# An attention block on one Trainium2 core: the masks of the probabilities' high and low parts in one GpSimd instruction for each key tile

## Chip, core and metric

The kernel runs on one core of a Trainium2 chip. The metric is the device time of one execution in microseconds (us), the median of the executions shown. The engines of the core are TensorE (PE in the rows, its weight loads PEld), VectorE (DVE), ScalarE (ACT), GpSimd (POOL) and SyncE (SP), which here only issues DMAs. Each works through its own program in order and waits for the others by semaphores.

## The reference

The block is a transformer layer with adaptive layer norm on x of shape (2, 1024, 512): attention with 32 query heads and 8 key heads of 128, rotary embedding and a sliding window of 128 keys, then a gated feed-forward part. The part that matters here:

```python
i = pos[:, None]
j = pos[None, :]
allowed = (j <= i) & (j > i - SLIDING_WINDOW)
scores = jnp.where(allowed[None, None, None], scores, neg)
attn = jax.nn.softmax(scores, axis=-1)
out = jnp.einsum('bhgqs,bshd->bqhgd', attn, v).reshape(B, S, N_Q_HEADS * HEAD_DIM)
```

## The kernel before

All matrix products are made in three passes: each fp32 operand is split into a high part, rounded to fp32r, and a low part, the rest; `mm3` (L276, L277, L278) multiplies high by high, high by low and low by high into one PSUM bank.

Attention is 16 **steps**, one for each batch and key head. A step is 8 **units**, one for each tile of 128 queries, with the 4 query heads of the group side by side (512 columns). Most steps run in a hardware loop whose body holds units 2 to 9; units 8 and 9 are units 0 and 1 of the next step. In unit u, TensorE does `scores(u)` (pS), `p_times_v(u-2)` (pAv), `trans(u-1)`, the transposes of the probabilities (pTr, L286), one or two projections of the next chunk of 512 tokens (`slot_jobs`, pP), `out_proj(u-2)` (pOp), and in units 3 and 7 `turn_v`, the transposes of V (pXx, L355). The work of a probability tile goes from engine to engine: TensorE scores, VectorE `merge` (L879 to L885), ScalarE `exps` (L641), GpSimd `normalise` (L1249), TensorE `trans`, ScalarE `p_hi` (L634, pT part 0), VectorE `p_lo` (L865, pT part 1), GpSimd `mask` (L1242, pm), TensorE `p_times_v`. ScalarE `result_hi` (L629) and VectorE `result_lo` (L860) split its product for `out_proj`.

A window of 128 keys covers two key tiles, so `mask` makes two copies of the probabilities: pm[:, 0] with the keys of the query's own tile up to the diagonal, pm[:, 1] with those of the tile before beyond it. Unit 0 has only the first. `pm` is [128, 2, 2, 4, 128] (tile, part, head, query), and `pT` is [128, 2, 4, 128] (part, head, query).

Beside this runs the rotary work of the coming chunk, a **job** for each of K, Q0 to Q3 and V. A rotary job is `swap` on ScalarE (L651, L652), `rope_cos` on VectorE (L895), `rope_sin` on GpSimd (L1255), `rope_sum` on VectorE (L901, both inputs in SBUF), `rope_hi` on ScalarE (L661) and `rope_lo` on VectorE (L912, both inputs in SBUF, counts the job into `j_done`). In units 3 and 7 the jobs' part of VectorE's program is: sum of Q2, sum of Q3, the reciprocal of the row sums (L890), low part of Q2, low part of Q3. `p_lo` stands right ahead of it. GpSimd's program in such a unit is `mask` and then `normalise`. The next unit of TensorE, 4 or 8, uses the new chunk, and its scores begin with

```python
f.wait(j_done, PER_J, JB - 1 + (6 if t >= CH else 0) + PER_J * (u // NT))
```

which is fulfilled by the low part of Q3. `split_weight` on VectorE (L1033) makes the low parts of the weights, also from two inputs in SBUF.

Of the kernel before, what the change touches and what calls it, by code (L numbers as in the profile page):

```python
# [24 lines left out]
P = 128  # L25
# [3 lines left out]
ALU = mybir.AluOpType  # L29
# [42 lines left out]
def adaln_block(nc, x, wq, wk, wv, wo, w12, b12, w3, b3, cond, wmod, cos, sin, x1_spill, out):  # L72
# [3 lines left out]
    G = wq.shape[1] // DH // NKV  # L76
# [9 lines left out]
    with ExitStack() as ctx:  # L86
# [7 lines left out]
        base = {}  # L94

        def sbr(name, shape, dt):
            base[name] = nc.sbuf_base
            return sb(name, shape, dt)
# [16 lines left out]
        pT = sbr("pT", [P, 2, G, P], F32R)  # L115
        pm = sbr("pm", [P, 2, 2, G, P], F32R)
# [1115 lines left out]
        def _(pool):  # L1232
            def mask(f, u):

                f.wait(u_plo, PER_U, u + 1)
                f.wait(u_av, PER_U, u)
                f.stand()
                for own in ((0, 1) if u % NT else (0,)):
                    for part in range(2):

                        sign, op = (1, ALU.is_ge) if own == 0 else (-1, ALU.is_gt)
                        last = nc.gpsimd.affine_select(out=pm[:, own, part], in_=pT[:, part], compare_op=op,  # L1242
                                                       fill=0.0, base=0, pattern=[[0, G], [sign, P]],
                                                       channel_multiplier=-sign)
                last.then_inc(u_mask, 1)

            def normalise(f, u):
# [26 lines left out]
            def unit_step(f, u, b, jobs, prev=True):  # L1274
                if prev:
                    mask(f, u - 1)
                normalise(f, u)
                jobs()
                if u == 4:
                    side_rstd(f)  # L1280
# [22 lines left out]
            def residual_bias(i):  # L1303
# [3 lines left out]
                else:  # L1307
# [10 lines left out]
                                    pattern=[[-1, P]], channel_multiplier=1).then_inc(s_const, 1)  # L1318
            nc.gpsimd.affine_select(out=rA[:, 2, 0:P], in_=rA[:, 2, 0:P], compare_op=ALU.is_ge, fill=0.0, base=0,
                                    pattern=[[-1, P]], channel_multiplier=1).then_inc(s_const, 1)  # L1320
            nc.gpsimd.affine_select(out=rA[:, 2, P:2 * P], in_=rA[:, 2, P:2 * P], compare_op=ALU.is_gt, fill=0.0,
                                    base=0, pattern=[[1, P]], channel_multiplier=-1).then_inc(s_const, 1)
# [21 lines left out]
            for b in range(B):  # L1344
# [19 lines left out]
                for u in range(2, NT):  # L1364
# [7 lines left out]
                    if b == 0 and u >= 4:  # L1372
                        clear_y(u - 4)
            fl = Frame(pool, STEPS)
            mask(fl, -1)
            finish(fl, -2, 1)
            finish(fl, -1, 1)
# [218 lines left out]
```

## Time and profile before

| | before |
| --- | --- |
| median of 3 runs | 1507.73 us (1504.65 to 1507.94) |
| profiled execution: time | 1505.94 us |
| profiled execution: span of its instructions | 1504.1 us |
| TensorE matmul busy | 1476.1 us (98%) |
| VectorE busy | 1103.5 us (73%) |
| GpSimd busy | 868.4 us (58%) |
| ScalarE busy | 823.2 us (55%) |
| masks on GpSimd (L1242) | 480 instructions, 392.3 us |

The profiled execution took 1.8 us more than its span. Busy times are unions of the instructions' own spans; consecutive instructions of one engine overlap in the records by some hundredths of a us. An instruction that has been started and waits for a port is counted as busy, so a long duration can hold a wait.

### The profile page before, as it was taken

Reading aid. Unit: us, or ns where it says so; the run is one execution under the profiler, and the core shown is the slowest. Engines: PE = TensorE matmul, PEld = TensorE weight load, DVE = VectorE, ACT = ScalarE, POOL = GpSimd, SP = SyncE. Lnnn points to the kernel's source line nnn. Section 1 sums busy time; section 2 is a strip of 40 time slices with the busy share of each in tenths; the row PEclk is TensorE's granted clock in tenths of the full one; section 3 lists DMA queues with packets and bytes.
Section 4 is the critical chain, followed back from the end, with each engine's and each line's share of the span. In section 5 each row is a group of like instructions: output and inputs, shape, how many; then the busy total and the mean of one; then the engine's idle time right before and its main releaser. Section 6 shows DMA issues by size and latency. Waiting matters only on the chain.

```text
span 1504.1 us, 27328 instructions
## 1 busy us (share of the span) xinstructions
PE 1476.1 (98%) x7577; PEld 1227.3 (82%) x7577; DVE 1103.5 (73%) x1849; ACT 823.2 (55%) x2183; POOL 868.4 (58%) x894
## 2 busy tenths in 40 slices
PE   6989999999999999999999999999999999999998
PEld 4578888888888888887888888888888888877887
DVE  6678787778787878788777878787877868773542
ACT  3555565656555656555565655565655556552331
POOL 2346565556565566669855656556664665675333
PEclk9999999999999999999999999999999999999999
DMA  9011110020201111324302020111111101153001
GB/s 315 21 36 57 36 56 28 18 73 7 72 18 56 35 56 35 104 71 134 106 16 77 7 70 21 56 35 56 35 56 35 56 28 38 60 182 127 28 29 56
DMA packets 98688, 90.20 MB, mean 60 GB/s; under 512 B 5450, under 2 KB 73042, under 8 KB 98646
## 3 DMA queue, kind: packets, MB, share of 16 engines
q1 hardware_dynamic: 97718, 87.06, 18.4%
q0 software_dynamic: 640, 2.10, 0.4%
q10 hardware_dynamic: 288, 0.53, 0.1%
q8 instruction: 21, 0.34, 0.1%
q14 instruction: 21, 0.17, 0.0%
HBM read 74.98 MB, written 14.69 MB: 60 GB/s over the span
## 4 chain that ended last, share of the span: by engine, by line
PE 87%; issue 4%; DVE 4%; POOL 3%; ACT 1%; DMA 1%; SPq 0%; POOLq 0%; DVEq 0%; ACTq 0%
PE pP L276 11%; PE pP L278 11%; PE pP L277 11%; PE pOp L276 8%; PE pOp L278 7%; PE pOp L277 7%; PE pS L278 4%; PE pAv L276 4%; PE pS L277 4%; PE pS L276 4%; PE pAv L277 4%; PE pAv L278 4%; PE pTr L286 3%; PE pXx L355 1%; POOL y L1310 1%
## 5 line engine op out<-in xcount | busy, mean ns | idle before, releaser
L1242 POOL TENSOR_SCALAR_AFFINE_SELECT pm<-pT 128x512 fp32r<-128x512 f32 x480 | 392.3, 850 | 477.8 <-DVE pT L865 477.7
L276 PE MATMUL pP<-hT,wp 128*128 128x512 f32 (+1 forms) x776 | 314.5, 405 | 6.9 <-DVE hT L998 4.0
L278 PE MATMUL pP<-hT,wp 128*128 128x512 f32 (+1 forms) x776 | 303.3, 391 | 0.0
L277 PE MATMUL pP<-hT,wp 128*128 128x512 f32 (+1 forms) x776 | 302.3, 390 | 0.0
L629 ACT CAST oT<-pAv 128x512 fp32r<-128x512 f32 x128 | 74.9, 585 | 283.8 <-PE pAv L278 283.8
L1255 POOL TENSOR_TENSOR rB<-rB,tab 128x512 f32<-128x512 f32 x160 | 218.3, 1376 | 16.3 <-ACT rB L652 16.2
L641 ACT ACTIVATE pr<-pS,nb 128x128 f32<-128x128 f32 x512 | 181.4, 371 | 63.3 <-DVE nb L885 63.2
L895 DVE TENSOR_TENSOR rA<-pP,tab 128x512 f32<-128x512 f32 x160 | 110.3, 689 | 131.0 <-ACT rB L652 131.0
L276 PE MATMUL pOp<-wos,oT 128*128 128x512 f32 x512 | 201.4, 393 | 3.7 <-DVE oT L860 3.4
L278 PE MATMUL pOp<-wos,oT 128*128 128x512 f32 x512 | 199.6, 390 | 0.0
L277 PE MATMUL pOp<-wos,oT 128*128 128x512 f32 x512 | 199.3, 389 | 0.0
L276 PEld LDWEIGHTS pP<-hT,wp 128*128 128x128 f32 x776 | 147.1, 190 | 33.5 <-DVE hT L998 4.1
L278 PEld LDWEIGHTS pP<-hT,wp 128*128 128x128 f32 x776 | 146.9, 189 | 32.0
L277 PEld LDWEIGHTS pP<-hT,wp 128*128 128x128 f32 x776 | 147.5, 190 | 26.6
L912 DVE TENSOR_TENSOR qT<-rA,qT 128x512 fp32r<-128x512 f32 x128 | 136.3, 1083 | 19.4 <-ACT qT L661 19.3
L1249 POOL TENSOR_TENSOR pr<-pr,rs 128x512 f32<-128x512 f32 x128 | 139.7, 1091 | 15.6 <-DVE rs L890 15.6
L276 PE MATMUL pS<-kv,qT 128*128 128x192 f32 (+2 forms) x512 | 142.0, 277 | 4.6 <-DVE grow L1112 4.3
L278 PE MATMUL pS<-kv,qT 128*128 128x192 f32 (+2 forms) x512 | 141.3, 276 | 0.0
L277 PE MATMUL pS<-kv,qT 128*128 128x192 f32 (+2 forms) x512 | 140.8, 275 | 0.0
L901 DVE TENSOR_TENSOR rA<-rA,rB 128x512 f32<-128x512 f32 x160 | 132.7, 870 | 0.0
L651 ACT COPY rB<-pP 64x512 f32<-64x512 f32 x160 | 93.4, 584 | 63.7 <-PE pP L278 61.3
L276 PEld LDWEIGHTS pOp<-wos,oT 128*128 128x128 f32 x512 | 96.1, 188 | 29.7 <-DVE oT L860 5.4
(187 smaller groups left out, 3016.1 us busy)
## 6 DMA issues: line engine op xcount, KB each, us to landing
st<-in_L_attn_wq_dram SPq DMA_DIRECT2D x64, 256.0 KB, 3.5
st<-in_L_attn_wo_dram SPq DMA_DIRECT2D x64, 256.0 KB, 3.7
h_dram<-hs SPq DMA_DIRECT2D x16, 512.0 KB, 3.9
st<-in_L_attn_wk_dram SPq DMA_DIRECT2D x16, 256.0 KB, 4.2
st<-in_L_attn_wv_dram SPq DMA_DIRECT2D x16, 256.0 KB, 2.6
wm<-in_L_wmod_dram SPq DMA_DIRECT2D x4, 1024.0 KB, 10.2
xin<-in_L_attn_x_dram SPq DMA_DIRECT2D x16, 256.0 KB, 3.1
qT<-h_dram SPq DMA_DIRECT2D x2, 2048.0 KB, 10.2
```

Source lines behind the costliest of these rows:

```text
L276: nc.tensor.matmul(o, hi_l, hi_r, start=start, stop=False, skip_group_check=True)
L277: nc.tensor.matmul(o, hi_l, lo_r, start=False, stop=False, skip_group_check=True)
L278: return nc.tensor.matmul(o, lo_l, hi_r, start=False, stop=stop, skip_group_check=True)
L629: nc.scalar.copy(oT[:, 0].rearrange("p h q -> p (h q)"), pAv[:]).then_inc(u_ohi, 1)
L641: last = nc.scalar.activation(pr[:, u % 2, i, :], pS[:, at:at + P], ACT.Exp, bias=nb[:, u % 2, i:i + 1], scale=SCALE, accum_out=sums[:, u ...
L651: nc.scalar.copy(rB[0:64, r, :], pP[j % 2][64:128, :])
L895: nc.vector.tensor_tensor(rA[:, j % 3, :], pP[j % 2][:], tab[:, 0, ch * CT:(ch + 1) * CT], ALU.mult).then_inc(r_cos, 1)
L901: nc.vector.tensor_tensor(rA[:, j % 3, :], rA[:, j % 3, :], rB[:, j % 3, :], ALU.add).then_inc(r_sum, 1)
L912: nc.vector.tensor_tensor(dst, src, hi, ALU.subtract).then_inc(j_done, 1)
L1242: last = nc.gpsimd.affine_select(out=pm[:, own, part], in_=pT[:, part], compare_op=op, fill=0.0, base=0, pattern=[[0, G], [sign, P]], chan ...
L1249: nc.gpsimd.tensor_tensor(pr[:, u % 2], pr[:, u % 2], rs[:, u % 2, :].unsqueeze(2).to_broadcast([P, G, P]), ALU.mult).then_inc(u_norm, 1)
L1255: nc.gpsimd.tensor_tensor(rB[:, j % 3, :], rB[:, j % 3, :], tab[:, 1, ch * CT:(ch + 1) * CT], ALU.mult).then_inc(r_sin, 1)
```

## The change

The loop over the two parts is gone. One `affine_select` takes both parts of pT (1024 elements a partition) and writes both parts of pm[:, own]; the pattern has one more dimension, of step 0, for the part. There are two such instructions a unit (one in unit 0) instead of four (two).

```diff
                 for own in ((0, 1) if u % NT else (0,)):
-                    for part in range(2):
-
-                        sign, op = (1, ALU.is_ge) if own == 0 else (-1, ALU.is_gt)
-                        last = nc.gpsimd.affine_select(out=pm[:, own, part], in_=pT[:, part], compare_op=op,
-                                                       fill=0.0, base=0, pattern=[[0, G], [sign, P]],
-                                                       channel_multiplier=-sign)
+                    sign, op = (1, ALU.is_ge) if own == 0 else (-1, ALU.is_gt)
+                    last = nc.gpsimd.affine_select(out=pm[:, own], in_=pT[:], compare_op=op, fill=0.0, base=0,
+                                                   pattern=[[0, 2], [0, G], [sign, P]], channel_multiplier=-sign)
                 last.then_inc(u_mask, 1)
```

The programs of TensorE, VectorE and ScalarE have the same rows before and after. GpSimd's program in unit 3, from the masks to the normalisation, before (REGISTER_ALU rows work out the values that semaphores are compared with; the waits stand in brackets):

```order
L58 REGISTER_ALU [waits u_plo]
L1242 AFFINE_SELECT pm<-pT 128x512 [waits u_av]
L1242 AFFINE_SELECT pm<-pT 128x512 x3
L58 REGISTER_ALU
L1249 TENSOR_TENSOR pr<-pr,rs 128x512 [waits u_rsum]
```

and the same place in the changed kernel, whose lines stand 2 to 3 higher:

```order
L58 REGISTER_ALU [waits u_plo]
L1240 AFFINE_SELECT pm<-pT 128x1024 [waits u_av]
L1240 AFFINE_SELECT pm<-pT 128x1024
L58 REGISTER_ALU
L1246 TENSOR_TENSOR pr<-pr,rs 128x512 [waits u_rsum]
```

Nothing changes its place: four instructions of 512 elements have become two of 1024, with the same waits ahead of the first and the same count behind the last.

VectorE's program of the same unit is as it was. From `p_lo` on it reads (the same rows before and after but for the numbers of lines, rows of registers left out):

```order
L865 TENSOR_TENSOR pT<-pTr,pT 128x512 [waits u_phi]
...
L901 TENSOR_TENSOR rA<-rA,rB 128x512 [waits r_cos]
...
L890 RECIPROCAL rs<-sums 128x4 [waits u_exp]
...
L912 TENSOR_TENSOR qT<-rA,qT 128x8x64 [waits r_hi]
```

The sum row stands there twice, for Q2 and for Q3, and so does the row of the low part. Nothing has moved.

## Rows read from the trace of the kernel before

**Rows 1.** The page, busy time of each engine.

```profile
PE 1476.1 (98%) x7577; PEld 1227.3 (82%) x7577; DVE 1103.5 (73%) x1849; ACT 823.2 (55%) x2183; POOL 868.4 (58%) x894
```

**Rows 2.** Groups of GpSimd: shapes, count, busy us, mean ns, idle before.

```profile
L1242 POOL TENSOR_SCALAR_AFFINE_SELECT pm<-pT 128x512 fp32r<-128x512 f32 x480 | 392.3, 850 | 477.8 <-DVE pT L865 477.7
...
L1317 POOL TENSOR_SCALAR_AFFINE_SELECT ident<-ident 128x128 f32<-128x128 f32 x1 | 0.3, 288 | 0.2 <-POOL rA L1314 0.2
```

**Rows 3.** Timeline of GpSimd in unit 4: one mask: start us, us, instruction.

```profile
1084.42 0.63 POOL L1242 TENSOR_SCALAR_AFFINE_SELECT pm<-pT 128x512 fp32r<-128x512 f32 x1 [6.18 <-DVE pT L865]
```

**Rows 4.** Timeline of VectorE, unit 3 of a step.

```profile
1072.95 0.68 DVE L901 TENSOR_TENSOR rA<-rA,rB 128x512 f32<-128x512 f32 x1
1073.55 1.12 DVE L901 TENSOR_TENSOR rA<-rA,rB 128x512 f32<-128x512 f32 x1
1074.68 1.03 DVE L912 TENSOR_TENSOR qT<-rA,qT 128x512 fp32r<-128x512 f32 x1
1075.63 1.11 DVE L912 TENSOR_TENSOR qT<-rA,qT 128x512 fp32r<-128x512 f32 x1
```

**Rows 5.** Timeline of GpSimd in the same unit.

```profile
1073.24 0.88 POOL L1242 TENSOR_SCALAR_AFFINE_SELECT pm<-pT 128x512 fp32r<-128x512 f32 x1 [2.32 <-DVE pT L865]
1074.08 1.08 POOL L1242 TENSOR_SCALAR_AFFINE_SELECT pm<-pT 128x512 fp32r<-128x512 f32 x1
...
1077.21 1.04 POOL L1249 TENSOR_TENSOR pr<-pr,rs 128x512 f32<-128x512 f32 x1
```

**Rows 6.** Timeline of TensorE, end of unit 3 and first scores of unit 4.

```profile
1076.86 0.60 PE L355 MATMUL pXx<-ident,rB 128*128 128x128 f32 x4
1077.21 0.34 PE L276 MATMUL pS<-kv,qT 128*128 128x192 f32 x1
```

**Rows 7.** The waits of the whole run: us in total, times, longest.

```profile
ACT kv L671 <- PE pXx L355: 52.8, 32, 2.5
...
PEld pOp L276 <- issue: 5.0, 14, 0.5
```

**Rows 8.** Timeline of unit 9: low parts on VectorE, normalisation on GpSimd.

```profile
1136.37 1.03 DVE L912 TENSOR_TENSOR kv<-rA,kv 128x512 fp32r<-128x512 f32 x1
1136.83 1.47 POOL L1249 TENSOR_TENSOR pr<-pr,rs 128x512 f32<-128x512 f32 x1
1137.33 1.53 DVE L912 TENSOR_TENSOR qT<-rA,qT 128x512 fp32r<-128x512 f32 x1
```

**Rows 9.** Timeline of unit 4: a weight's low part beside `rope_sin`.

```profile
1089.03 1.29 POOL L1255 TENSOR_TENSOR rB<-rB,tab 128x512 f32<-128x512 f32 x1
1089.22 1.64 DVE L1033 TENSOR_TENSOR wp<-st,wp 128x512 fp32r<-128x512 f32 x1
```

**Rows 10.** Timeline: low parts, and scores that waited for them.

```profile
710.66 2.07 DVE L912 TENSOR_TENSOR qT<-rA,qT 128x512 fp32r<-128x512 f32 x2
...
712.78 0.30 PE L276 MATMUL pS<-kv,qT 128*128 128x64 f32 x1 [0.27 <-DVE qT L912]
```

**Rows 11.** Timeline: TensorE in unit 5, then the masks and TensorE in unit 6.

```profile
1094.14 0.39 PE L277 MATMUL pP<-hT,wp 128*128 128x512 f32 x1
1094.36 0.39 PE L278 MATMUL pP<-hT,wp 128*128 128x512 f32 x1
1094.63 0.49 PE L276 MATMUL pOp<-wos,oT 128*128 128x512 f32 x1
1094.96 0.39 PE L277 MATMUL pOp<-wos,oT 128*128 128x512 f32 x1
...
1095.22 4.00 POOL L1242 TENSOR_SCALAR_AFFINE_SELECT pm<-pT 128x512 fp32r<-128x512 f32 x4 [3.95 <-DVE pT L865]
...
1099.13 0.28 PE L278 MATMUL pS<-kv,qT 128*128 128x192 f32 x1
1099.35 0.50 PE L276 MATMUL pAv<-pm,kv 128*128 128x512 f32 x1
1099.68 0.40 PE L277 MATMUL pAv<-pm,kv 128*128 128x512 f32 x1
```

## The prediction

> **What bounds the kernel now.** I read the page's busy times first. TensorE is busy 98% of the span, VectorE 73%, GpSimd 58% [rows 1]. So an engine other than TensorE can cost time only where TensorE waits for it, and can give back only what TensorE waits for it now, which is little. The masks are GpSimd's largest group, 392.3 us, and GpSimd is idle for 477.8 us ahead of them, waiting for `p_lo` [rows 2]: it has time to spare, and taking work off it is worth nothing by itself. The question is when the masks end, and whom GpSimd keeps waiting meanwhile.
>
> For that I read the timelines of GpSimd and VectorE side by side in one unit. The reader is to see that the same instruction has two lengths. A mask alone takes 0.63 us [rows 3]; in unit 3 it takes 1.08, while on VectorE `rope_sum`, 0.68 when nothing holds it, takes 1.12, and `rope_lo` 1.03 and 1.11 [rows 4, 5]. They take turns. The first mask ends at 1074.12; the second sum, begun at 1073.55, ends 0.55 later, at 1074.67. The second mask, begun at 1074.08, ends 0.49 after that, at 1075.16. The first low part ends 0.55 later, at 1075.71. Each waits until the other engine's instruction is over, and then needs about 0.5 us. A longer GpSimd instruction makes it wait longer: a low part on VectorE that begins at 1089.22 beside a `rope_sin` of 1.29 that ends at 1090.32 ends 0.54 after it, at 1090.86 [rows 9]. So what is shared is held for a whole GpSimd instruction, and the two engines alternate instruction by instruction. The Trainium skill says the same (SBUF — State Buffer, Who interferes with whom): a VectorE instruction with two SBUF inputs and a GpSimd instruction that reads SBUF exclude each other for the whole instruction. The trace agrees, by the 0.54 after the 1.29.
>
> Last I looked for who waits for the end of this exchange. The second low part of unit 3 ends at 1076.74 [rows 4] and the scores of unit 4 begin at 1077.21 [rows 6]. They need that job. Where TensorE did wait for it, the scores began 0.05 after its end (712.73 and 712.78) [rows 10]. So only 0.47 - 0.05 = 0.42 us is free there. Unit 7 and the scores of unit 8 are built alike. `turn_v` marks these places: ScalarE waited 32 times for its transposes [rows 7]; one is the prologue's, so there are 31.
>
> **The change, part by part.** It takes 240 instructions off GpSimd.
>
> *The price of one.* 128 columns take 0.288, 512 take 0.63 [rows 2, 3]: (0.63 - 0.288)/384 = 0.89 ns a column, so 512 more are 0.46, and a mask of 1024 alone takes 1.09. No row shows 1024 columns or the fourth dimension. From below I bound it by the slope alone, 0.91; from above by two separate masks, 1.26. I take 1.09, since two points of the same operation give it.
>
> *The turns in unit 3, anew.* First mask: 0.88 + 0.46 = 1.34, to 1074.58. Second sum: 0.55 later, 1075.13 (before 1074.67). Second mask: 0.49 + 0.46 = 0.95 later, 1076.08. It is the last, so the masks are ready 1.1 earlier than before, when the instruction behind them began at 1077.21. First low part: it can begin at 1075.14, is held up by the second mask, ends 0.55 after it, 1076.63. And now the normalisation comes in. Before, its turn came at 1077.21, behind both low parts [rows 4, 5]. Now GpSimd issues it at about 1076.04, ahead of the second low part (about 1076.55), so it takes the next turn. Unit 9, where there are two masks already, shows this order: the normalisation ends at 1138.30, 0.90 after the first low part (1137.40), and the second low part ends 0.56 after that, having taken 1.53 [rows 8]. So: normalisation to 1077.53, second low part to 1078.09. That is 1.35 later than 1076.74. In words: of the two turns that two masks gave up, VectorE gets nothing, because both merged masks are longer and a normalisation of 1 us has moved ahead of the low part that TensorE needs next.
>
> *What TensorE pays.* 1.35 - 0.42 = 0.93 us at a place. In three of the 31 the free time is gone already (rows 10 is one); there it is the full 1.35. 28 x 0.93 + 3 x 1.35 = 30.1 us. Nothing gives it back within the unit: `p_lo`, which starts the exchange, follows `result_lo` and `p_hi`, which follow TensorE's own `p_times_v`, so a late TensorE makes the next exchange late as well. Behind the second low part on VectorE stand the split of weights (unit 3) or the sum into y (unit 7), which can be late without TensorE waiting.
>
> *The same delay elsewhere.* In units 5 and 9 VectorE also comes out of the exchange late, by no more than the same 1.35. Who needs those low parts (of K and Q0) is three units away; next late is `result_lo`, and its `out_proj` stands behind 24 projection matmuls. VectorE has 27% idle time to catch up in [rows 1]. I cost it at nothing; if that cover were gone, it would be up to 1 us more at some 30 places.
>
> *What TensorE gains.* In unit 6 `p_times_v` begins when the masks of unit 5 (4.00 us from 1095.22) are done: it begins 0.22 after the last matmul of the scores, 192 columns wide, and the next one 0.33 later, where 512 columns take 0.22 (1094.14 to 1094.36). By that width the first step should be about 0.1, the second 0.22: 0.2 us too much [rows 11]. These masks come 1.1 sooner, so it goes: 0.2 x 14 regular steps = 2.8. In unit 5 `out_proj` is held up too, 0.27 and 0.33 between starts, 0.15 over [rows 11]; the wait list has it 14 times [rows 7]. It hangs on `result_lo`, behind the split of a weight that waits for `rope_sin` of unit 4 [rows 9], and that comes earlier by what the undisturbed masks of unit 4 save, at most two fixed parts of 0.63 - 0.46 = 0.17, some 0.3. With TensorE itself late it vanishes anyway: 0.15 x 14 = 2.1. Irregular places between the batches and in the last step, where POOL or VectorE is late, may give 1 to 2, say 1.6. Together 6.5.
>
> *The sum:* 30.1 - 6.5 = 23.6 us on a span of 1504.1, so 1527.7, and with the 1.8 around it 1529.5 for an execution like the profiled one (1505.94). The median shown is 1.8 above that execution: 1531.3.
>
> **The rivals.**
>
> *Shorter masks, and nothing else (faster).* If the second low part keeps its turn ahead of the normalisation, it ends 0.55 after the first, at 1077.18: 0.44 late against 0.42 free, a stall of nothing, and the 6.5 us remain: 1501. The place is the one turn behind the second mask; the rival decides from the moment that GpSimd issues the normalisation later than VectorE its low part, which would take a gap of 0.5 us behind a mask of two parts. For it: a rule of turns that I infer. Against it: unit 9 shows the other order [rows 8], and GpSimd's instructions follow each other without a gap [rows 5]. The saving of one instruction is its fixed part, 0.17, and all of it falls on an engine with idle time. The Trainium skill (GPSIMD Engine Reference, 2.1 Instruction dispatch) puts that part down to a software dispatch for each instruction; the 0.17 agree with it in kind.
>
> *The instruction is dearer.* Each x us more for one mask delays the low part by 2x, at 31 places. With 1.26 (x = 0.17) that is 10.5 us more: 1542. With a body that goes over columns more slowly in four dimensions it would be more still; at 1.5 us, 25 more, 1557. The other bound, 0.91, gives 11 less: 1520.
>
> *The two orders mixed (no change).* With 6.5 us of gains, the loss cancels at 6.5/31 = 0.21 a place, a low part 0.63 late instead of 1.35. That is a mean between the two orders, 0.44 and 1.35: the normalisation would have to come first at a fifth of the places only. The units 3 and 7 repeat with the same starts to some hundredths, which speaks for one order at all.
>
> **How the numbers follow.** The exchange as worked out, with the bounds of the mask's price, has 0.75: 1520 to 1542. A much dearer mask has 0.06. The orders mixed with mine the more frequent, 1512 to 1520, has 0.06. Within 0.2%, which is about what a measurement of this kernel tells from no change, 0.05. The faster rival 0.08. So slower by over 0.2%: 0.87, same 0.05, faster 0.08. The time is that of the first case, 1531, and the range that leaves out no more than 2 in 10 is 1517 to 1543.
>
> **What would show it.** In the changed kernel's trace: masks of 1024 columns at 1.09 alone and about 1.34 and 1.54 in the exchange; in units 3 and 7 the low parts at about 1.5 each instead of 1.03 and 1.11, with the normalisation ending between them; TensorE idle before the first scores of units 4 and 8, put down to `rope_lo`, some 0.9 us at 28 places; no extra step before `p_times_v` in unit 6. VectorE's busy time rises though its program is the same. I am wrong if the normalisation ends after the second low part, if the scores follow it without a wait, or if a mask of 1024 columns alone is far from 1.1.

## The result and the profile after

The changed kernel takes 1530.88 us, the median of 4 runs (1530.06 to 1532.77), against 1506.19 (1503.71 to 1507.94) before: a ratio of 1.0165 (95% interval 1.0148 to 1.0183), some 25 us slower. That is the way and the size of the forecast, 1531. It meets it to the microsecond by chance: 23.6 us had been worked out and 24.7 were measured, and the forecast stood on a median before of 1507.73, which is 1506.19 with a fourth execution.

The page of the changed kernel, busy time of each engine (answers to [rows 1]):

```profile
span 1531.0 us, 27088 instructions
...
PE 1478.3 (97%) x7577; PEld 1229.5 (80%) x7577; DVE 1140.7 (75%) x1849; ACT 824.2 (54%) x2183; POOL 803.4 (52%) x654
```

GpSimd has 65 us less to do and 240 instructions fewer. VectorE, whose program is the same, is busy 37 us longer: that is time in which its instructions stand started and wait. The chain that ended last went 87% through TensorE before; now:

```profile
PE 73%; DVE 11%; issue 10%; POOL 2%; ACT 2%; DMA 1%; DVEq 0%; SPq 0%; POOLq 0%; ACTq 0%
...
PE pP L276 9%; PE pP L278 9%; PE pP L277 9%; PE pOp L276 6%; PE pOp L278 6%; PE pOp L277 6%; DVE qT L912 5%; PE pS L276 4%; PE pS L278 4%; PE pS L277 4%; PE pAv L276 4%; PE pAv L278 4%; PE pAv L277 4%; PE pTr L286 3%; DVE rA L901 2%
```

`rope_lo` (L912) has come into it. The mask's line, ns of one (minimum, median, maximum), and the wait list:

```profile
L1240 POOL TENSOR_SCALAR_AFFINE_SELECT pm<-pT x240: 1088/1343/1575, 73.4 to 1386.1; 128x1024 fp32r<-128x1024 f32 x120
```

```profile
PEld pS L276 <- issue: 33.8, 30, 5.3
...
PE pS L276 <- DVE qT L912: 24.0, 31, 1.2
```

A mask of 1024 columns alone takes 1.09 us, its lowest. TensorE now waits for `rope_lo` ahead of the scores 31 times, at each of the places that the prediction counted. The first line is the same wait, as the weight loads have it, at 28 of them (before it stood at 6.1 us in 2 places): there the wait stands on a register instruction ahead of the weight load, and the list calls that "issue". The time of 24.0 is measured from modelled ends of matmuls; by starts it is more (below).

Unit 3 of one step, VectorE, then GpSimd (line 1246 is the normalisation), then TensorE. These answer to [rows 4], [rows 5] and [rows 6]; the same step starts 21.38 us later here:

```profile
1094.33 0.68 DVE L901 TENSOR_TENSOR rA<-rA,rB 128x512 f32<-128x512 f32 x1
1094.92 1.58 DVE L901 TENSOR_TENSOR rA<-rA,rB 128x512 f32<-128x512 f32 x1
...
1096.52 1.49 DVE L912 TENSOR_TENSOR qT<-rA,qT 128x512 fp32r<-128x512 f32 x1
1097.93 1.52 DVE L912 TENSOR_TENSOR qT<-rA,qT 128x512 fp32r<-128x512 f32 x1
```

```profile
1094.62 1.34 POOL L1240 TENSOR_SCALAR_AFFINE_SELECT pm<-pT 128x1024 fp32r<-128x1024 f32 x1 [2.58 <-DVE pT L865]
1095.92 1.55 POOL L1240 TENSOR_SCALAR_AFFINE_SELECT pm<-pT 128x1024 fp32r<-128x1024 f32 x1
1097.43 1.47 POOL L1246 TENSOR_TENSOR pr<-pr,rs 128x512 f32<-128x512 f32 x1
```

```profile
1098.23 0.60 PE L355 MATMUL pXx<-ident,rB 128*128 128x128 f32 x4
1099.58 0.35 PE L276 MATMUL pS<-kv,qT 128*128 128x192 f32 x1 [0.75 <-DVE qT L912]
```

Read the ends in order: mask 1095.96, sum 1096.50, mask 1097.47, low part 1098.01, normalisation 1098.90, low part 1099.45, scores 1099.58. From the first sum's start to the end of the second low part it is 5.12 us, against 3.79 before (1072.95 to 1076.74) [rows 4]. TensorE's transposes begin at 1098.23 and the scores follow 1.35 later, where they followed 0.35 later before (1076.86, 1077.21) [rows 6]: TensorE loses 1.00 us here.

In unit 6 the last matmul of the scores and the first ones of `p_times_v` (answers to [rows 11]) stand 0.12 and 0.25 apart, not 0.22 and 0.33: that wait for the masks is gone.

```profile
1121.30 0.28 PE L278 MATMUL pS<-kv,qT 128*128 128x192 f32 x1
1121.42 0.42 PE L276 MATMUL pAv<-pm,kv 128*128 128x512 f32 x1
1121.67 0.40 PE L277 MATMUL pAv<-pm,kv 128*128 128x512 f32 x1
```

### The profile page after: what moved, and what is told of

It is laid out like the page before. It is cut to its first block, busy times and chain, and to the rows that moved or that the text cites. A ratio compares the mean times of both kernels' runs of the same rounds, so it can differ in the third digit from the quotient of the medians.

```text
span 1531.0 us, 27088 instructions
## 1 busy us (share of the span) xinstructions
PE 1478.3 (97%) x7577; PEld 1229.5 (80%) x7577; DVE 1140.7 (75%) x1849; ACT 824.2 (54%) x2183; POOL 803.4 (52%) x654
## 4 chain that ended last, share of the span: by engine, by line
PE 73%; DVE 11%; issue 10%; POOL 2%; ACT 2%; DMA 1%; DVEq 0%; SPq 0%; POOLq 0%; ACTq 0%
PE pP L276 9%; PE pP L278 9%; PE pP L277 9%; PE pOp L276 6%; PE pOp L278 6%; PE pOp L277 6%; DVE qT L912 5%; PE pS L276 4%; PE pS L278 4%; PE pS L277 4%; PE pAv L276 4%; PE pAv L278 4%; PE pAv L277 4%; PE pTr L286 3%; DVE rA L901 2%
## 5 line engine op out<-in xcount | busy, mean ns | idle before, releaser
L1240 POOL TENSOR_SCALAR_AFFINE_SELECT pm<-pT 128x1024 fp32r<-128x1024 f32 x240 | 314.0, 1330 | 537.4 <-DVE pT L865 537.2
L1252 POOL TENSOR_TENSOR rB<-rB,tab 128x512 f32<-128x512 f32 x160 | 212.7, 1342 | 27.8 <-ACT rB L652 27.8
L912 DVE TENSOR_TENSOR qT<-rA,qT 128x512 fp32r<-128x512 f32 x128 | 170.3, 1349 | 19.8 <-ACT qT L661 19.3
L1246 POOL TENSOR_TENSOR pr<-pr,rs 128x512 f32<-128x512 f32 x128 | 158.4, 1238 | 26.4 <-DVE rs L890 26.4
L276 PE MATMUL pS<-kv,qT 128*128 128x192 f32 (+2 forms) x512 | 142.5, 278 | 28.4 <-DVE qT L912 24.0
L901 DVE TENSOR_TENSOR rA<-rA,rB 128x512 f32<-128x512 f32 x160 | 158.4, 1031 | 0.0
L276 PEld LDWEIGHTS pS<-kv,qT 128*128 128x128 f32 x512 | 98.3, 192 | 40.4 <-issue 33.8
```

The source lines that it names most:

```text
L276: nc.tensor.matmul(o, hi_l, hi_r, start=start, stop=False, skip_group_check=True)
L901: nc.vector.tensor_tensor(rA[:, j % 3, :], rA[:, j % 3, :], rB[:, j % 3, :], ALU.add).then_inc(r_sum, 1)
L912: nc.vector.tensor_tensor(dst, src, hi, ALU.subtract).then_inc(j_done, 1)
L1240: last = nc.gpsimd.affine_select(out=pm[:, own], in_=pT[:], compare_op=op, fill=0.0, base=0, pattern=[[0, 2], [0, G], [sign, P]], channel_ ...
L1246: nc.gpsimd.tensor_tensor(pr[:, u % 2], pr[:, u % 2], rs[:, u % 2, :].unsqueeze(2).to_broadcast([P, G, P]), ALU.mult).then_inc(u_norm, 1)
L1252: nc.gpsimd.tensor_tensor(rB[:, j % 3, :], rB[:, j % 3, :], tab[:, 1, ch * CT:(ch + 1) * CT], ALU.mult).then_inc(r_sin, 1)
```

## The experiments

The theory to test: on the path lies the second low part of units 3 and 7, and it is late because it waits in turn for GpSimd instructions, each for its whole length, and the merged masks let the normalisation come ahead of it. Each of the following kernels ran beside the kernel before on its own chip: median 1506.21 for the first four, 1506.39 for the last three. The places of the argument are the 31 ahead of the scores of units 4 and 8.

**1. The normalisation behind the low parts.** Edit, on the changed kernel (the condition leaves out the last step's second half, where no rotary job runs; the call, not shown, passes `b`):

```diff
-            def normalise(f, u):
+            def normalise(f, u, b):
+                if u % CH == 3 and not (f.regs is None and b == 1 and u >= CH):
+                    f.wait(j_done, PER_J, JB + (0 if u % NT < CH else 6) + PER_J * (u // NT) + SLOT["Q3"] + 1)
                 f.wait(u_rsum, PER_U, u + 1)
```

> The changed kernel, but in units 3 and 7 the normalisation also waits for the low part of Q3. My theory (the normalisation takes the turn between the two low parts): the second low part ends 0.55 after the first, some 0.45 later than before instead of 1.35, the scores of units 4 and 8 wait for it by under 0.1 us, and the gains elsewhere remain: 1500 to 1504 us, ratio to before 0.996 to 0.999. Rival A (the longer hold of two masks of 1024 columns is enough, 0.46 each, whatever follows): the low part stays 0.9 late, a stall of 0.5 at 31 places, 1515 to 1518. Rival B (the masks themselves are late for TensorE): as the changed kernel, 1531.

Measured: 1507.09 us (1505.11 to 1508.26), ratio 1.0006 (0.9997 to 1.0015). So 24 of the 25 us are back, with the merged masks in every unit. Rivals A and B are out. It is 3 us above my own range. The timelines of VectorE, GpSimd and TensorE in unit 3:

```profile
1074.85 1.48 DVE L912 TENSOR_TENSOR qT<-rA,qT 128x512 fp32r<-128x512 f32 x1
1076.25 0.68 DVE L912 TENSOR_TENSOR qT<-rA,qT 128x512 fp32r<-128x512 f32 x1
...
1077.10 1.04 POOL L1248 TENSOR_TENSOR pr<-pr,rs 128x512 f32<-128x512 f32 x1 [1.31 <-DVE qT L912]
...
1076.57 0.60 PE L355 MATMUL pXx<-ident,rB 128*128 128x128 f32 x4
1077.06 0.35 PE L276 MATMUL pS<-kv,qT 128*128 128x192 f32 x1
```

The first low part is as slow as in the changed kernel, the second takes its undisturbed 0.68. It ends at 1076.93 and the scores begin at 1077.06, 0.13 later and 0.49 behind the start of the transposes instead of 0.35: still a stall of 0.14. From the low part to the scores it is 0.13 us here, not the 0.05 that I read off [rows 10], so less was free than I counted. At the other places in the loop the stall is up to 0.22, and over all 31 it is 6.5 us.

**2. Merged everywhere but in units 3 and 7.** On the changed kernel:

```diff
                 for own in ((0, 1) if u % NT else (0,)):
                     sign, op = (1, ALU.is_ge) if own == 0 else (-1, ALU.is_gt)
-                    last = nc.gpsimd.affine_select(out=pm[:, own], in_=pT[:], compare_op=op, fill=0.0, base=0,
-                                                   pattern=[[0, 2], [0, G], [sign, P]], channel_multiplier=-sign)
+                    if u % CH != 2:
+                        last = nc.gpsimd.affine_select(out=pm[:, own], in_=pT[:], compare_op=op, fill=0.0, base=0,
+                                                       pattern=[[0, 2], [0, G], [sign, P]],
+                                                       channel_multiplier=-sign)
+                        continue
+                    for part in range(2):
+                        last = nc.gpsimd.affine_select(out=pm[:, own, part], in_=pT[:, part], compare_op=op,
+                                                       fill=0.0, base=0, pattern=[[0, G], [sign, P]],
+                                                       channel_multiplier=-sign)
```

Here u is the unit of the masks, which are worked on one unit later, in unit 3 or 7.

> The changed kernel, but the masks worked on in units 3 and 7 are four instructions of 512 columns again; in all other units they stay merged. My theory: the exchange of units 3 and 7 is as before, no stall ahead of the scores of units 4 and 8, and the gains of the shorter masks elsewhere (6.5 us by my sum) are seen alone: 1499 to 1503. Rival C (a merged instruction costs wherever it stands, for instance in the exchanges of units 5 and 9): slower than before, 1510 or more.

Measured: 1500.26 us (1499.70 to 1502.22), ratio 0.9963 (0.9949 to 0.9976), 6 us faster than before. Rival C is out: a merged mask does no harm elsewhere, and the gains that I summed to 6.5 are there. This is the fastest version of all. It has 176 merged instructions in place of 352, and 128 as before:

```profile
L1241 POOL TENSOR_SCALAR_AFFINE_SELECT pm<-pT 128x1024 fp32r<-128x1024 f32 x176 | 223.3, 1289 | 409.2 <-DVE pT L865 409.1
```

**3. Merged in units 3 and 7 alone**, the kernel of experiment 2 with the condition turned round.

```diff
-                    if u % CH != 2:
+                    if u % CH == 2:
```

> The other part alone: merged masks in units 3 and 7, four instructions of 512 everywhere else. My theory: the whole loss is here, 30 us, and a part of the gains comes with a late TensorE anyway, so 1530 to 1536. Rival C: about half of the loss, 1515 to 1522.

Measured: 1534.61 us (1533.61 to 1535.82), ratio 1.0189 (1.0173 to 1.0205). The whole loss sits in these 31 places (the masks of 32 units), and a little more than in the full change, since the gains elsewhere are missing.

**4. One merged, two split in units 3 and 7**, against experiment 2:

```diff
-                    if u % CH != 2:
+                    if u % CH != 2 or own == 0:
```

> The changed kernel, but in units 3 and 7 the masks are one instruction of 1024 columns and then two of 512, three turns instead of two. My theory (what counts is whose turn comes between the low parts): the third mask stands between them and the normalisation behind them, the second low part is 0.46 late against 0.42 free, nearly no stall: 1500 to 1505, though this kernel has merged masks in every unit. Rival A': each merged mask has half of the loss, 0.46 to 0.68 at each place, so 1512 to 1520.

Measured: 1505.17 us (1504.59 to 1507.19), ratio 0.9995 (0.9986 to 1.0004), 0.2 above my range and far below the rival's. VectorE's second low part, the third mask and the normalisation on GpSimd, TensorE:

```profile
1076.09 1.11 DVE L912 TENSOR_TENSOR qT<-rA,qT 128x512 fp32r<-128x512 f32 x1
...
1075.59 1.07 POOL L1246 TENSOR_SCALAR_AFFINE_SELECT pm<-pT 128x512 fp32r<-128x512 f32 x1
1076.64 1.46 POOL L1253 TENSOR_TENSOR pr<-pr,rs 128x512 f32<-128x512 f32 x1
...
1076.86 0.60 PE L355 MATMUL pXx<-ident,rB 128*128 128x128 f32 x4
1077.33 0.35 PE L276 MATMUL pS<-kv,qT 128*128 128x192 f32 x1
```

With a third turn for a mask the normalisation comes behind the second low part, which ends at 1077.20, 0.46 later than before, as worked out, and the scores follow 0.13 later again.

**5. The normalisation in two halves** in units 3 and 7, on the changed kernel.

```diff
-                nc.gpsimd.tensor_tensor(pr[:, u % 2], pr[:, u % 2],
-                                        rs[:, u % 2, :].unsqueeze(2).to_broadcast([P, G, P]), ALU.mult
-                                        ).then_inc(u_norm, 1)
+                for h in ((0, 2) if u % CH == 3 else (0,)):
+                    n = 2 if u % CH == 3 else G
+                    last = nc.gpsimd.tensor_tensor(pr[:, u % 2, h:h + n], pr[:, u % 2, h:h + n],
+                                                   rs[:, u % 2, h:h + n].unsqueeze(2).to_broadcast([P, n, P]), ALU.mult)
+                last.then_inc(u_norm, 1)
```

> The changed kernel, but the normalisation of units 3 and 7 is two instructions of two heads each. My theory (the low part waits for one whole GpSimd instruction): only the first half stands between the two low parts, half of its 0.9 us, so the second low part comes some 0.45 us earlier at 31 places and 14 us come back: 1515 to 1519. Rival D (the order of the two engines is fixed by the wait behind the masks, not by the length of what stands between): 1531 as the changed kernel.

Measured: 1519.67 us (1517.32 to 1520.02), ratio 1.0077 (1.0061 to 1.0092): 11 us back of the 14 expected, 0.7 above my range. Rival D, which has 1531, is out: what stands between the low parts costs by its length. The low parts on VectorE, the first half on GpSimd, the scores:

```profile
1086.57 2.51 DVE L912 TENSOR_TENSOR qT<-rA,qT 128x512 fp32r<-128x512 f32 x2
...
1087.48 1.04 POOL L1248 TENSOR_TENSOR pr<-pr,rs 128x256 f32<-128x256 f32 x1
...
1089.20 0.35 PE L276 MATMUL pS<-kv,qT 128*128 128x192 f32 x1 [0.32 <-DVE qT L912]
```

The first half ends at 1088.52, the low part 0.56 later at 1089.08.

**6. Control: the kernel before with the wait of experiment 1.** On the kernel before (signature and call as in experiment 1, not shown):

```diff
+                if u % CH == 3 and not (f.regs is None and b == 1 and u >= CH):
+                    f.wait(j_done, PER_J, JB + (0 if u % NT < CH else 6) + PER_J * (u // NT) + SLOT["Q3"] + 1)
                 f.wait(u_rsum, PER_U, u + 1)
```

> A control: the kernel before (four masks of 512 everywhere), with the wait of the first experiment ahead of the normalisation of units 3 and 7. There the normalisation comes behind both low parts anyway. My theory: no change, 1505 to 1508. Rival E (the added wait on GpSimd costs by itself, which would be why the first experiment gave 1507 and not 1502): 1510 or more.

Measured: 1506.26 us (1504.95 to 1508.28), ratio 0.9998 (0.9989 to 1.0007). The added wait costs nothing by itself, so rival E is out. The 7 us between experiments 1 and 2 are what the late low part still costs: in the trace of experiment 1 TensorE waits 6.5 us more at the 31 places than before, in that of experiment 2 nothing more.

**7. The masks behind the low parts** in units 3 and 7, all merged: the wait of experiment 1 stands ahead of the masks instead of the normalisation (signature and call not shown).

```diff
+                if u % CH == 2 and not (f.regs is None and b == 1 and u >= CH):
+                    f.wait(j_done, PER_J, JB + (0 if u % NT < CH else 6) + PER_J * (u // NT) + SLOT["Q3"] + 1)
                 f.wait(u_plo, PER_U, u + 1)
```

> The changed kernel, merged masks everywhere, but in units 3 and 7 they wait for the low part of Q3, so that the two engines don't take turns there. My theory: sums and low parts run undisturbed, the second low part ends some 1 us earlier than before the change, TensorE never waits for it; the masks take 2.15 undisturbed and are ready some 0.7 us before TensorE wants them: 1499 to 1505, about as the second experiment. If the masks or what comes behind them are too late instead: 1508 or more.

Measured: 1502.96 us (1502.51 to 1504.38), ratio 0.9974 (0.9963 to 0.9986). VectorE, GpSimd and TensorE in unit 3:

```profile
1072.30 1.29 DVE L912 TENSOR_TENSOR qT<-rA,qT 128x512 fp32r<-128x512 f32 x2
...
1073.88 2.14 POOL L1242 TENSOR_SCALAR_AFFINE_SELECT pm<-pT 128x1024 fp32r<-128x1024 f32 x2 [5.24 <-DVE qT L912]
...
1074.84 0.60 PE L355 MATMUL pXx<-ident,rB 128*128 128x128 f32 x4
1075.19 0.34 PE L276 MATMUL pS<-kv,qT 128*128 128x192 f32 x1
```

Taken apart, the exchange vanishes: both low parts together take 1.29, are done at 1073.59, and 1.60 us are free ahead of the scores. The masks take 2.14, as estimated. Yet it is 2.7 us slower than experiment 2 (2.5 by the difference of each from its own kernel before; the intervals of the two ratios overlap). Part of that is seen one unit and a half later, where `out_proj` in unit 5 still begins late (0.30 and 0.33 between starts, as in [rows 11]):

```profile
1092.34 0.39 PE L278 MATMUL pP<-hT,wp 128*128 128x512 f32 x1
1092.64 0.49 PE L276 MATMUL pOp<-wos,oT 128*128 128x512 f32 x1
1092.97 0.40 PE L277 MATMUL pOp<-wos,oT 128*128 128x512 f32 x1
```

The two traces put 2.5 us there, over 14 regular places, and 1.1 us at two places between the batches, where `p_times_v` begins later than in experiment 2. They also show what keeps `out_proj` late, though I did not test it by an edit. Behind the late masks the normalisation is late as well, and the split of a weight, which comes next on VectorE, runs into it:

```profile
1075.99 1.04 POOL L1248 TENSOR_TENSOR pr<-pr,rs 128x512 f32<-128x512 f32 x1
1076.61 0.96 DVE L1033 TENSOR_TENSOR wp<-st,wp 128x512 fp32r<-128x512 f32 x1 [3.02 <-ACT wp L624]
```

It takes 0.96 instead of 0.69, at each of the 15 places of this kind (0.93 to 0.99), and it ends 0.54 after the normalisation. From there on VectorE is later: from the first scores of unit 4 to `result_lo` of unit 5 it is 16.53 us (1075.19 to 1091.72), against 16.25 in experiment 2, and `out_proj` waits for `result_lo`.

## Why the prediction was right

**What bounds the kernel.** Right. TensorE has the same work, and the time moved by what it waits.

**The price of a mask.** 1.09 alone, as taken (1088 ns, the minimum); the fourth dimension costs nothing that shows. In the exchange 1.34 and 1.55, predicted 1.34 and 1.54. The bounds of 0.91 and 1.26 were not needed.

**The turns.** Right in order, at 30 of the 31 places, and in size. The second low part was predicted 1.35 later within the exchange and is 1.33 later (5.12 against 3.79). Experiments 1 and 4 put the normalisation behind it in two ways, and nearly the whole loss went; experiment 5 halved what stands between, and nearly half of it went; experiment 7 took the exchange away, and the loss went. That an instruction with two SBUF inputs on VectorE is held for the whole of the GpSimd instruction ahead of it is what SBUF — State Buffer (Who interferes with whom) in the Trainium skill states; the ends 0.54 to 0.56 after masks, normalisation and half normalisation bear it out.

The 31st place lies between the two batches, in the changed kernel and in experiments 1 and 5. GpSimd clears a tile of y first, its masks begin late, and the second mask takes the turn between the two low parts:

```profile
723.93 1.56 POOL L1240 TENSOR_SCALAR_AFFINE_SELECT pm<-pT 128x1024 fp32r<-128x1024 f32 x1
724.46 1.58 DVE L912 TENSOR_TENSOR qT<-rA,qT 128x512 fp32r<-128x512 f32 x1
725.46 1.48 POOL L1246 TENSOR_TENSOR pr<-pr,rs 128x512 f32<-128x512 f32 x1
```

**What TensorE pays.** There are errors of size here, which nearly cancel. The free time was not 0.42 but 0.47 - 0.13 = 0.34. The 0.05 of [rows 10] was right for that place, one of three outside the hardware loop, and wrong for the 28 in it. Outside, the weight load itself waits and starts 0.05 behind the low part. In the loop the wait stands on a register instruction that works out the value of the next wait: in the changed kernel the low part ends at 1099.45, that instruction starts at 1099.49, and the weight load and the scores at 1099.58. In the traces of the changed kernel and of experiments 1, 3, 4 and 5 alike, 28 places show 0.13 and three 0.05. So a regular place costs 1.00, not 0.93: 2 us more over 28. The three irregular places cost about 1.1, 0.9 and 1.1 (the scores start 1.13, 1.48 and 1.13 after the last transpose, and before the change 0.04, 0.54 and 0.06), not 1.35: 1 us less. Summed over the 31 places from the last transpose to the first scores, it is 32.4 us after and 1.4 before: 31.0, predicted 30.1.

The same sum from one trace of each kernel, beside the medians, both as differences from the kernel before, in us:

| kernel | median | time from last transpose to scores, 31 places |
| --- | --- | --- |
| changed | +24.7 | +31.0 |
| experiment 1 | +0.9 | +6.5 |
| experiment 2 | -5.9 | 0.0 |
| experiment 3 | +28.4 | +31.4 |
| experiment 4 | -1.0 | +5.7 |
| experiment 5 | +13.3 | +18.2 |
| experiment 6 | -0.1 | 0.0 |
| experiment 7 | -3.4 | -0.5 |

What the median lies below the sum is gained elsewhere: 5 to 7 us in the changed kernel and in experiments 1, 2, 4 and 5, 3 in experiments 3 and 7, nothing that shows in the control.

**What TensorE gains.** Predicted 6.5. Experiment 2, in which nothing is lost at the 31 places, shows 5.9 (1506.21 to 1500.26), and 31.0 less the 24.7 between the medians leaves 6.3. The wait for the masks in unit 6 vanished. By the starts of the matmuls in experiment 2, `p_times_v` gains 2.3 us in the loops (predicted 2.8), `out_proj` 2.9 (predicted 2.1), and the places between the batches and in the last step 0.6, where 1.6 had been taken without a row.

**The rivals.** The faster one had its threshold in the right place: with the low part ahead of the normalisation the second low part is 0.48 and 0.46 late in experiments 1 and 4, predicted 0.44. But by the true 0.34 the stall is 0.1 to 0.2 rather than nothing, and the time 1505 to 1507 rather than 1501. The mixture of orders didn't occur: the normalisation comes first at 30 of the 31 places, and all of them show the wait.

## What to carry to other kernels

Before merging small instructions on GpSimd, look in both timelines for VectorE instructions with two SBUF inputs beside them: the two engines take turns by whole instructions, and fewer, longer ones on one side give the other side fewer turns and bring up sooner whatever stands next in the first engine's queue. Find out which instruction TensorE waits for behind such an exchange, measure its free time from the end of the producer to the start of the consumer less the answer time of the semaphore, taken at a place with the same code around the wait (here 0.13 in the loop, 0.05 outside), and merge only where that is larger than what you add. Here 128 of the 480 masks left as they were turned 25 us lost into 6 us won.

## What the runs showed of the hardware

In the hardware loop, where a second wait with a register value follows the first, TensorE's matmul starts 0.13 us after the end of the VectorE instruction that releases it (1099.45 to 1099.58 after the change, 1076.93 to 1077.06 in experiment 1, 1077.20 to 1077.33 in experiment 4). Outside the loop it is 0.05 at all three places, also where TensorE had waited for over 1 us (726.04 to 726.09 after the change).

An engine that comes early can collide anew. In experiment 2, `side_lo` on VectorE (L1028, two SBUF inputs) in unit 7 takes 1.24 us, beside a `rope_sin` that now overlaps it, where it took 0.79 before:

```profile
1105.35 1.24 DVE L1028 TENSOR_TENSOR hs<-hm,hs 128x512 fp32r<-128x512 f32 x1 [0.41 <-ACT hs L731]
```

```profile
1104.76 1.28 POOL L1259 TENSOR_TENSOR rB<-rB,tab 128x512 f32<-128x512 f32 x1
```

Everything behind it on VectorE is later, and its second low part of unit 7 ends (1110.72 + 2.06 = 1112.78) 0.26 us ahead of the scores of unit 8 (1113.04) instead of the 0.46 of the kernel before. It is still enough: 0.13 of it is the answer, and 0.13 is left before TensorE waits.
